# First group's loads in halves, constants reordered, the last group's result in three parts: a gated attention and mixture-of-experts kernel

## The reference

```python
# per sequence of 64 tokens (K = ctx, Q = layernorm(x)):
scores = jnp.einsum('btd,bsd->bts', K, K) * tril          # no softmax
x = x + tanh(g_xattn) * (Q + einsum('bts,bsd->btd', scores, Q))
# per token of the new x, n = layernorm(x):
shared = silu(n @ shared_w1.T) @ shared_w2.T              # hidden 512
logits = n @ gate_w.T                                     # 8 experts, the top 2
gates  = softmax over the top 2, 0 elsewhere
expert_out[e] = silu(n @ experts_w1[e].T) @ experts_w2[e].T
x = x + tanh(g_ffn) * (shared + sum_e gates[e] * expert_out[e])
```

## Time and profile before

| | us |
|---|---|
| median of 3 runs | 228.30 |
| lowest and highest | 228.19, 228.93 |
| the profiled execution | 228.44 |
| its span in the profile | 226.6 |
| busy: PE, PEld | 220.6, 191.6 |
| busy: POOL, ACT, DVE | 147.6, 133.0, 118.0 |

### The profile page before, as it was taken

How to read it: one execution, slowest core, us unless ns; L and a number is a source line. 1 busy time by engine, 2 the same in 40 slices (tenths; PEclk the granted TensorE clock), 3 DMA queues, 4 the chain that set the end, 5 groups by cost and what they waited for, 6 DMA issues and landing times.

```text
span 226.6 us, 5999 instructions
## 1 busy us (share of the span) xinstructions
PE 220.6 (97%) x1728; PEld 191.6 (85%) x1731; DVE 118.0 (52%) x546; ACT 133.0 (59%) x304; POOL 147.6 (65%) x178
## 2 busy tenths in 40 slices
PE   7989999999999999999999999999999999999993
PEld 2754867786777789999999999999999999999793
DVE  6899998856864589995203210221122102466214
ACT  2649896597475555655565556545654565466510
POOL 4772875767777777777777777777744544465600
PEclk9999999999999999999999999999999999999998
DMA  6899210211245995867774266777777776999633
GB/s 233 263 392 392 66 54 33 64 52 52 68 98 156 260 285 161 228 185 183 197 202 151 72 196 202 215 238 223 219 244 220 200 228 187 271 355 370 238 95 127
DMA packets 30478, 43.47 MB, mean 192 GB/s; under 512 B 4992, under 2 KB 16512, under 8 KB 30192
## 3 DMA queue, kind: packets, MB, share of 16 engines
q1 hardware_dynamic: 25264, 32.87, 49.0%
q0 software_dynamic: 4320, 9.41, 11.4%
q10 hardware_dynamic: 864, 0.80, 1.0%
HBM read 30.45 MB, written 12.62 MB: 190 GB/s over the span
## 4 chain that ended last, share of the span: by engine, by line
PE 90%; DMA 3%; DVE 2%; ACT 1%; POOL 1%; issue 1%; POOLq 0%; SPq 0%; DVEq 0%; ACTq 0%
PE bank L1343 28%; PE bank L1364 28%; PE bank L1191 11%; PE bank L1204 10%; PE bank L1317 3%; PE bank L1138 3%; PE bank L1145 2%; DMA y_rows<-y,dest 2%; PE bank L1122 2%; PE bank L1211 2%; PE bank L1155 1%; DMA q<-y_rows 1%; PE bank L1115 1%; POOL rstd L492 0%; POOL y_rows L557 0%
## 5 line engine op out<-in xcount | busy, mean ns | idle before, releaser
L557 POOL DMA_INDIRECT y_rows<-y,dest x71 | 69.7, 982 | 36.6 <-ACT y L733 25.1
L531 POOL DMA_INDIRECT expert_rows<-n,slot x64 | 62.8, 981 | 24.3 <-issue 18.3
L1364 PE MATMUL bank<-w,hT 128*128 x568 | 74.5, 275 | 0.0
L1343 PE MATMUL bank<-xT,w_ring 128*128 128x128 f32 (+1 forms) x432 | 74.1, 309 | 0.0
L1364 PEld LDWEIGHTS bank<-w,hT 128*128 128x128 f32 x568 | 71.3, 192 | 1.6
L727 ACT ACTIVATE hT<-bank 128x512 f32<-128x512 f32 x71 | 42.4, 597 | 34.3 <-PE bank L1343 34.2
L1343 PEld LDWEIGHTS bank<-xT,w_ring 128*128 128x128 f32 x432 | 59.3, 192 | 2.0 <-issue 0.2
L1024 DVE COPY xT<-bank 128x512 f32<-128x512 f32 (+2 forms) x19 | 12.4, 653 | 72.3 <-PE bank L1317 72.3
L733 ACT ACTIVATE y<-bank,gate 128x128 f32<-128x128 f32 x71 | 26.1, 368 | 21.3 <-PE bank L1364 20.9
L1204 PEld LDWEIGHTS bank<-sw,sT 128*128 128x128 f32 x224 | 27.4, 192 | 5.3 <-issue 5.0
L1191 PE MATMUL bank<-nT,sw 128*128 128x512 f32 x56 | 28.7, 609 | 0.0
(11 more groups left out here) (154 smaller groups left out, 198.1 us busy)
## 6 DMA issues: line engine op xcount, KB each, us to landing
w_ring<-in_w1T SPq DMA_DIRECT2D x54, 256.0 KB, 3.6
x_ring<-expert_rows SPq DMA_DIRECT2D x37, 72.5 KB, 2.8
x_ring<-expert_rows SPq DMA_DIRECT2D x17, 145.0 KB, 3.7
w<-in_w2T SPq DMA_DIRECT2D x2, 1024.0 KB, 11.8
kT<-y_rows SPq DMA_DIRECT2D x8, 256.0 KB, 6.5
nT<-y_rows SPq DMA_DIRECT2D x7, 256.0 KB, 4.5
out<-xres SPq DMA_DIRECT2D x7, 256.0 KB
xres<-in_xP SPq DMA_DIRECT2D x3, 512.0 KB, 7.1
```

The costliest lines, as they stand in the source:

```text
L531: pool.indirect_dma_start(out=x_dram[:, :], out_offset=bass.IndirectOffsetOnAxis(ap=slot[:, i, k:k + 1], axis=0), in_=n[:, i, :], in_offse ...
L557: pool.indirect_dma_start(out=y_dram[:, :], out_offset=bass.IndirectOffsetOnAxis(ap=dest[:, b:b + 1], axis=0), in_=y[:, j], in_offset=None ...
L1343: last = pe.matmul(ps_up(b)[:, j * width:(j + 1) * width], w1_ring[:, w % W_RING, c * P:(c + 1) * P], xT[:, s % X_SETS, i * P:i * P + widt ...
L1364: last = pe.matmul(ps_y(b), hidden(b, c), w2[:, ds(at + c * D, D)], start=(c == 0), stop=(c == HC - 1))
```

## The change

- SP asks for the tokens of group 0 in two DMAs of 256 columns, with semaphores `x_first` and `x_in[0]`. `statistics1(0)` waits for the first half before tile 0 and for the second before tile 2.
- ACT asks for the context of group 0 in two DMAs, `ctx_first` and `ctx_in[0]`. `start_score(0)` doesn't wait for context any more; `score_tile(0, 0)` waits for the first half and `score_tile(0, 2)` for the second.
- POOL writes `ident4` first and signals it alone (`ident4_ready`); `start_score(0)` waits for that, and `consts_ready` is waited for in `transpose_n(0)` and `mask_scores(0)`.
- The 128 x 2175 memset of `pad` leaves DVE. ACT writes the zeros after its table load, in five copies of 3 pad rows from `warm` (128 x 3 x 137), and POOL waits for them (`pad_zeroed`) before it numbers the pad rows. DVE still writes the -1 columns of `pad`.
- `keep_warm(8)` becomes `keep_warm(6)`.
- The last group's shared result goes into three banks: tiles 0 and 1, tile 2, tile 3. DVE adds it in three instructions (256, 128 and 128 columns); ACT stores the first, SP the other two.

```diff
@@ LAST, banks @@
+    PAD_ROWS = 3
-        ps_last_sup, ps_last_so = [bank[1], bank[2], bank[5], bank[6]], [bank[1], bank[2]]
+        ps_last_sup, ps_last_so = [bank[1], bank[2], bank[5], bank[6]], [bank[1], bank[2], bank[5]]
+        def part_of(t):
+            return max(0, t - 1)
+        def part_cols(part):
+            return slice(0, 2 * D) if part == 0 else slice((part + 1) * D, (part + 2) * D)
@@ SP @@
-            load_tokens(0)
+            sp.dma_start(xres[:, 0:GW // 2], xP[:, 0:GW // 2]).then_inc(x_first, 16)
+            sp.dma_start(xres[:, GW // 2:GW], xP[:, GW // 2:GW]).then_inc(x_in[0], 16)
             load_tokens(1)
             load_context(2)
             sp.wait_ge(x_in[1], 16)
...
-            sp.wait_ge(last_added, 2)
-            sp.dma_start(outP[:, last_cols(1)], xres[:, last_cols(1)]).then_inc(stored, 16)
-            sp.wait_ge(stored, 16 * (GROUPS + 1))
+            for part in range(1, 3):
+                sp.wait_ge(last_added, part + 1)
+                sp.dma_start(outP[:, LAST * GW:][:, part_cols(part)], xres[:, LAST * GW:][:, part_cols(part)]).then_inc(stored, 16)
+            sp.wait_ge(stored, 16 * (GROUPS + 2))
@@ POOL @@
+            chained(pool.memset(ident4[:, :, :], 0.0))
+            pool.affine_select(out=ident4[:, :, :], in_=ident4[:, :, :], compare_op=ALU.not_equal, fill=1.0,
+                               base=0, pattern=[[0, G], [-1, P]], channel_multiplier=1).then_inc(ident4_ready, 1)
             chained(pool.memset(minus_half[:, :], -0.5))
...
                 pool.wait_ge(cleared, 1)
+                pool.wait_ge(pad_zeroed, PADS // PAD_ROWS)
@@ ACT @@
-            act.dma_start(kT[:, 0:GW], ctxT[:, 0:GW]).then_inc(ctx_in[0], 16)
+            act.dma_start(kT[:, 0:GW // 2], ctxT[:, 0:GW // 2]).then_inc(ctx_first, 16)
+            act.dma_start(kT[:, GW // 2:GW], ctxT[:, GW // 2:GW]).then_inc(ctx_in[0], 16)
...
             act.preload_act_table(ACT.Silu)
+            act.wait_ge(warm_ready, 1)
+            for i in range(0, PADS, PAD_ROWS):
+                act.activation(pad[:, i:i + PAD_ROWS, 0:AT], warm[:, 0:PAD_ROWS * AT].rearrange("p (i d) -> p i d", d=AT), ACT.Copy)\
+                    .then_inc(pad_zeroed, 1)
@@ DVE @@
+                    if (g, which, t) == (0, 0, G // 2):
+                        dve.wait_ge(x_in[0], 16)
...
-                dve.wait_ge(x_in[load_of[g]], 16)
+                dve.wait_ge(x_in[load_of[g]] if g else x_first, 16)
...
-            dve.memset(expert_step[:, :], 1.0)
-            chained(dve.memset(pad[:, :, :], 0.0))
+            chained(dve.memset(expert_step[:, :], 1.0))
...
-            def add_last_shared(half):
-                cols = last_cols(half)
-                dve.wait_ge(half_done, GROUPS + 1 + half)
-                dve.wait_ge(sdown_done, GROUPS + half)
+            def add_last_shared(part):
+                cols = part_cols(part)
+                dve.wait_ge(half_done, GROUPS + 1 + (part > 0))
+                dve.wait_ge(sdown_done, GROUPS + part)
...
             add_last_shared(1)
+            add_last_shared(2)
@@ PE @@
-                pe.wait_ge(ctx_in[ctx_load_of[g]], 16)
                 if g == 0:
-                    pe.wait_ge(consts_ready, 1)
+                    pe.wait_ge(ident4_ready, 1)
+                else:
+                    pe.wait_ge(ctx_in[ctx_load_of[g]], 16)
...
+                if g == 0 and t == 0:
+                    pe.wait_ge(ctx_first, 16)
+                if g == 0 and t == G // 2:
+                    pe.wait_ge(ctx_in[0], 16)
...
+                if g == 0:
+                    pe.wait_ge(consts_ready, 1)
                 at_least(pe, strips_done, g)
...
-            keep_warm(8)
+            keep_warm(6)
...
-                if t % (G // 2) == G // 2 - 1:
+                if t > 0:
                     last.then_inc(sdown_done, 1)
```

More of the change, by code:

```diff
@@ L232, in flamingo_gated_moe @@
         gT_in = sem("gT_in")
+        x_first = sem("x_first")
+        ctx_first = sem("ctx_first")
+        ident4_ready = sem("ident4_ready")
+        pad_zeroed = sem("pad_zeroed")
         x_in = [sem(f"x_in{i}") for i in range(len(LOADS))]
@@ L479, in _ @@
                                        base=0, pattern=[[-1, P]], channel_multiplier=1))
-            chained(pool.memset(ident4[:, :, :], 0.0))
-            chained(pool.affine_select(out=ident4[:, :, :], in_=ident4[:, :, :], compare_op=ALU.not_equal, fill=1.0,
-                                       base=0, pattern=[[0, G], [-1, P]], channel_multiplier=1))
             chained(pool.memset(mask[:, :], 1.0))
@@ L1074, in add_last_half @@
                     .then_inc(half_done, 1)
-            def add_last_shared(half):
-                cols = last_cols(half)
-                dve.wait_ge(half_done, GROUPS + 1 + half)
-                dve.wait_ge(sdown_done, GROUPS + half)
-                dve.scalar_tensor_tensor(out=xres[:, cols], in0=ps_last_so[half][:, half_cols(half)], scalar=tanh_g[:, 1:2],
-                                         in1=xres[:, cols], op0=ALU.mult, op1=ALU.add).then_inc(last_added, 1)
+            def add_last_shared(part):
+                cols = part_cols(part)
+                dve.wait_ge(half_done, GROUPS + 1 + (part > 0))
+                dve.wait_ge(sdown_done, GROUPS + part)
+                dve.scalar_tensor_tensor(out=xres[:, LAST * GW:][:, cols], in0=ps_last_so[part][:, cols], scalar=tanh_g[:, 1:2],
+                                         in1=xres[:, LAST * GW:][:, cols], op0=ALU.mult, op1=ALU.add).then_inc(last_added, 1)
             def add_late_shared():
@@ L1405, in _ @@
             for t in range(G):
-                half = t // (G // 2)
                 cols = slice(t * P, (t + 1) * P)
@@ L1410, in _ @@
                         pe.wait_ge(sT_done, HC * LAST + c + 1)
-                    last = pe.matmul(ps_last_so[half][:, cols], sT[:, LAST % 2, c, cols], sw2[:, c * D:(c + 1) * D],
+                    last = pe.matmul(ps_last_so[part_of(t)][:, cols], sT[:, LAST % 2, c, cols], sw2[:, c * D:(c + 1) * D],
                                      start=(c == 0), stop=(c == HC - 1))
-                if t % (G // 2) == G // 2 - 1:
+                if t > 0:
                     last.then_inc(sdown_done, 1)
```

## The result

The changed kernel is slower: 231.83 us (median of 4, 230.81 to 232.88) against 228.40 us for the kernel before, a ratio of 1.0142 with a 95% interval of [1.0113, 1.0171]. The prediction was 228.2 us, with a range of 227.6 to 229.0.

The account below looks back on a forecast made before the run. PE was taken to bound the kernel (busy 97%), leaving only front and tail to change: 228.44 - 0.11 + 0.05 = 228.38 us against the profiled execution, 228.24 against the median, rounded to 228.2; range 227.6 to 229.0.

Parts of the forecast that it names:

- Front: the loads behind: Loads queued behind group 0's, group 6's context included: delayed 0 by bytes to 0.43 us by issues, taken as 0.05.
- Rival D: Start: halves delay group 1's tokens by an issue (0.43 us), transpose at 14.28, total 228.7 to 229.0 us; chance 0.15.
- The estimate from the skill's figures: DMA engines: by a straight line between the skill's times, a pair of halves needs some 0.6 us more than one whole.
- rival C: PE at the start: idle makes its clock rise later, slowing scores and `apply_scores(0)` by 1.0 to 1.1 us, 229.3; chance 0.13.
- `keep_warm(6)` at no cost: PE's start: six products of zeros end 0.9 us earlier than eight, `score(0)` some 0.8 us earlier; no cost in the sum.
- rival A: First transpose: group 6's context, through its identity on PE, limits the front's gain; total 228.2 us; chance 0.52.
- the forecast's 0.11 us for the front: Up to the first transpose: it moves from 14.01 to 13.90 us, not by the 0.25 to 0.8 its steps gain.
- Statistics and `q`: Group 0's token chain on DVE: 0.35 us earlier (0 to 0.43), `var_eps` near 5.45, `q` near 7.05.
- The copies of `pad`: ACT's five copies at the start: 0.5 us each, ending at 6.9 (6.5 to 7.4), hidden ahead of `q`.
- Tail: End of the kernel: last store issued 0.2 us later with half the bytes; +0.05 us taken, from -0.15 to +0.2.

Follow-up runs that it names:

- d1_small: Kernel before plus one unused 4 KB DMA on each of the two queues, between group 0's and group 1's loads: 231.82 us, ratio 1.0144.
- f1_delay: Kernel before with group 1's and later loads on both queues issued later (group 1's at 1.71 instead of 1.24 us), no DMA more: 231.03 us, ratio 1.0081.
- a1_whole: Changed kernel with group 0's tokens and context each in one DMA again, six products of zeros kept: 228.33 us, ratio 0.9982 to the kernel before.
- b2_whole_warm8: Changed kernel with group 0's tokens and context whole and eight products of zeros: 227.56 us, ratio 0.9951 to the kernel before.
- u1_front: Kernel before with only the identity first and `pad` cleared by ACT; whole loads, eight products of zeros, last result in two parts: 228.41 us, ratio 0.9987.
- f3_third_late: Kernel before with only the third and later loads of both queues issued at 2.29 instead of 1.72 us, group 1's at 1.24 as before: 229.56 us, ratio 1.0019.
- t1_tail: Kernel before with only the last result in three parts: 228.26 us, ratio 0.9974.
- e2_small_after: Changed kernel with the small DMAs of the gates and `gT` issued only when ACT's five `pad` copies are done: 233.23 us, ratio 1.0206 to the kernel before.
- g1_ctx_later: Changed kernel with SP's 512 KB of context issued only when group 0's tokens are in: 232.11 us, ratio 1.0133 to the kernel before.
- b1_halves: Kernel before with only group 0's tokens and context in halves, and their waits: 230.70 us, ratio 1.0087.
- a2_x_whole: Changed kernel with group 0's tokens whole and only the context in halves: 231.19 us, ratio 1.0121 to the kernel before.
- e1_small_late: Changed kernel with the small DMAs of the gates and `gT` placed behind ACT's `pad` copies, without a wait: 232.45 us, ratio 1.0150 to the kernel before.

## Why the prediction was wrong

**The step that failed is "Front: the loads behind".** It saw that each queue has one issue more ahead of group 1's load, and bounded the delay by 0 (by bytes) and 0.43 us (by issues); it took 0.05, since the DMA engines were busy anyway. Both ends were too low. The load landed 2.46 us later for tokens and 2.30 for context. The bound by issues was right only for twelve of the 16 parts. The step treated a DMA as one thing that lands at issue plus a time; it lands with its last part, and d1_small and f1_delay show that three or four parts of a load issued 0.47 us later may land 2 us later. That "by bytes nothing changes" was no argument: d1_small moved 4 KB more a queue and lost as much. Rival D had the direction (halves delay the loads, "the transpose at 14.28, 228.7 to 229.0"), and was short by a factor of ten on the transpose (0.27 against 3.05 us). It stood beside rival C as an alternative, and the run had both, the delay and by it the clock. The estimate from the skill's figures, 0.6 us more of the engines, was nearer but is not what happened: f1_delay carries not one byte or DMA more.

**The clock, rival C.** Its mechanism came, as a consequence: not because PE had 0.4 us of idle before the first rise, but because it idled 2.83 us behind a `score(0)` that was now early. The granted clock rose at 4.95 (6.83 before), PE ran dry at 5.28, and the clock was low from 8.36 to 11.78. C's price, 1.0 to 1.1 us, is what the profile shows (1.10). Near to its own form, with six products of zeros and loads on time, it was seen in a1_whole's profile (the rise at 10.68, the transpose at 15.44). The sum had `keep_warm(6)` at no cost; a1_whole against b2_whole_warm8 is 0.9982 against 0.9951, which points at one, but the two intervals overlap.

**Group 6's context as a cap, rival A.** In the change it doesn't limit (its identity stands at 16.34, the transpose at 17.06 waits for `n`). In u1_front and b2_whole_warm8, with loads on time, it doesn't either: tokens that come whole land at 4.2, so the token chain is hardly earlier, and the transposes stand at 14.01 and 13.96 behind `n`. The cap itself was seen in f1_delay, and in f3_third_late, where that identity started at 13.67 behind its load and the transpose, at 14.11, right behind it. So the forecast's 0.11 us for the front was near to what the front gives without halves (0 to 0.05), but the limit that I named for it wasn't the one at work.

**Statistics and `q`.** `var_eps` at 5.11 instead of 5.45: the second half of the tokens landed at 4.08, and 4.40 was the earliest that I had allowed. The copies of `pad` took 0.46 each and ended at 6.75, below 7.0 as said. The 0.7 us that this chain gained were worth nothing, because group 1's loads were what the chain behind it waited for.

**Tail.** I gave it +0.05 us, with -0.15 and +0.2 as ends. t1_tail measured 0.9974, about -0.6 us. In the changed kernel's profile that gain isn't there: the span ends 3.58 us behind PE's last product (3.45 before), so 0.13 later, within my ends. Its rows are what I expected of the slow side: three adds back to back, and the last issue 0.3 us later against PE's end than before:

```profile
225.59 0.99 DVE L1100 SCALAR_TENSOR_TENSOR xres<-bank,tanh_g,xres 128x256 f32<-128x256 f32 x3
...
226.36 1.03 SPq L477 DMA_DIRECT2D out<-xres  x2
```

The gain in t1_tail comes with the earlier rows and the earlier store of group 6, a step that I hadn't in the sum at all.

**What stays open.** Why some parts of a load issued at 1.71 us or later are held until 7.2 to 8.4. It needs no bytes, no DMA and no half load more ahead (f1_delay), and no small packets behind (e2_small_after). Whether the 512 KB behind them take part is open: without them nothing came behind 7 us (g1_ctx_later), but with them b1_halves had its loads in by 6.54 too. The last parts end near the same time for issues at 1.71 and at 2.29, as if something held them until a fixed time. But no DMA engine stands still at that time in every program: with group 1's loads issued at 1.24, the 16 parts of the 512 KB came in between 6.45 and 7.19 (before) and between 6.54 and 7.56 (f3_third_late, issued at 2.29). The changed kernel's trace has no fetch of instructions between 0 and 14 us, so code loading isn't it. The engines were far from full when the late parts landed. The Trainium skill, same page, section "Latency and other measured facts", gives the memory's latency as 0.2 us on average and 2 us at high load, which would fit the size; no run here shows which it was.

## What to carry to other kernels

At the start of a kernel the load that the second stage waits for should be issued as early as it can be: cutting the first stage's load in halves buys its stage 0.7 us and can cost the next one 2, since a DMA lands with the last of its 16 parts and one issue later can mean several late parts. Before an engine is given its work earlier, ask what it does when that work is done: an idle PE ahead of late data pays a second time, in its clock. The part of this change that measured a gain is the last result in three parts: alone it gave 0.9974 [0.9955, 0.9993], and with whole loads, eight products of zeros, the identity first and `pad` on ACT 0.9951 [0.9932, 0.9970].

## What I had not expected of the hardware

- A load of 256 KB issued at 1.24 us landed by 5.77 in 14 of 14 cases, one issued at 1.71 or later at 5.95 to 8.37 in 22 of 22, also when nothing but the issue time differed (7.57 against 5.43 in f1_delay).
- A DMA of 4 KB between two loads, on each of two queues, cost the program as much as the whole change with its 256 KB in halves: 1.0144 against 1.0142.
- With the two queues out of step, a load landed right behind twice its bytes on the other queue: 7.79 us beside 7.6 (a2_x_whole).
- ACT's DMA issues ran ahead of copies written before them: issued at 3.51 and 3.88 us, when the last of the five copies ended at 5.78 (e1_small_late). So the strict order on an engine holds for its own work, and not for when its queue's issues go out.
- An idle time of 2.83 us on PE was followed by 3.4 us at 1.2 GHz that began 0.25 us after the work had come back (8.11, 8.36).
